# A state space stage: the weighted sums over 16 states, shared between ScalarE, an accumulating transfer and VectorE

## The reference

```python
xz = einsum('bld,ed->ble', x, W_in); u, z = split(xz, 2)
uc = silu(conv3(u) + conv_b)
x_dbl = einsum('blh,eh->ble', uc, W_xproj)          # dt part (64), B (16), C (16)
dt = softplus(einsum('blr,hr->blh', dtp, W_dt) + b_dt)
A = -exp(A_log)
def step(h, (u_t, dt_t, B_t, C_t)):
    dA = exp(dt_t[:, None, :] * A[None, :, None])
    h = dA * h + B_t[:, :, None] * u_t[:, None, :]
    y_t = einsum('bn,bnh->bh', C_t, h)               # the sum over 16 states
y = (scan(step) + D * uc) * silu(z)
out = einsum('blh,dh->bld', y, W_out)
```

## Time and profile before

| | |
|---|---|
| median of 3 runs | 3569.99 us (3563.14 to 3570.53) |
| span of the profiled execution | 3547.4 us |
| what lies around the span (median less span) | 22.6 us |
| DVE, PE, POOL, ACT busy, 200 to 800 us | 591.5, 533.8, 523.9, 472.0 us |
| the stage | 0 to about 910 us |

### The profile page before, as it was taken

How to read it: one execution, slowest core, us unless ns; L and a number is a source line. 1 busy time by engine, 2 the same in 40 slices (tenths; PEclk the granted TensorE clock), 3 DMA queues, 4 the chain that set the end, 5 groups by cost and what they waited for, 6 DMA issues and landing times. The chain is left out here.

```text
span 3547.4 us, 59663 instructions
## 1 busy us (share of the span) xinstructions
PE 3336.7 (94%) x21120; PEld 2437.0 (69%) x21120; DVE 2409.3 (68%) x5247; ACT 1564.9 (44%) x3124; POOL 1736.2 (49%) x2205
## 2 busy tenths in 40 slices
PE   7888988888589999999999989999999999999999
PEld 5666666666468888888876656666655566666565
DVE  8999999999655555555554447777733377777332
ACT  6887778876242222222221125555511255555111
POOL 6988889888450000000012237777611277777221
PEclk9999999999789999999999999999999999999999
DMA  4011101111441000010012211112121111121121
GB/s 143 1 62 62 62 1 62 62 56 46 146 125 37 13 10 13 10 37 12 12 36 74 81 60 37 37 37 60 30 74 54 60 32 38 37 72 31 61 65 35
DMA packets 166972, 176.13 MB, mean 50 GB/s; under 512 B 22756, under 2 KB 150264, under 8 KB 166296
## 3 DMA queue, kind: packets, MB, share of 16 engines
q1 hardware_dynamic: 163272, 162.94, 14.2%
q0 software_dynamic: 3408, 9.38, 0.7%
HBM read 94.19 MB, written 78.09 MB: 49 GB/s over the span
## 5 line engine op out<-in xcount | busy, mean ns | idle before, releaser
L3087 ACT ACTIVATE win_probs<-win_sc,win_nbias,tile_rn 128x256 f32<-128x256 f32 x512 | 282.3, 561 | 311.7 <-DVE win_nbias L3171 311.7
L438 POOL TENSOR_TENSOR ssm_acc<-ssm_acc,ssm_weighted 128x512 f32<-128x512 f32 x255 | 339.0, 1339 | 101.4 <-ACT ssm_weighted L587 100.7
L424 POOL TENSOR_SCALAR ssm_ub<-ssm_uT,ssm_bcT 128x512 f32<-128x512 f32 x512 | 359.1, 725 | 21.8 <-PE ssm_pu L1151 18.0
L1151 PEld LDWEIGHTS ssm_pu<-ident,ssm_ub 128*128 128x128 f32 x2048 | 237.6, 142 | 184.9 <-issue 87.0
L3273 PE MATMUL win_pa<-win_w_wqkv,tile_hT 128*128 128x512 f32 x744 | 360.9, 622 | 0.0
L1151 PE MATMUL ssm_pu<-ident,ssm_ub 128*128 128x128 f32 x2048 | 308.4, 279 | 51.0 <-DVE ssm_state L821 33.8
L1998 POOL TENSOR_TENSOR lin_rstd<-lin_mv,lin_eps 128x1 f32<-128x1 f32 x30 | 5.7, 190 | 667.5 <-DVE lin_mv L173 667.5
L1167 PE MATMUL ssm_pt<-ident,ssm_state 128*128 128x128 f32 x2040 | 278.1, 278 | 48.4 <-DVE ssm_acc L831 30.3
L821 DVE TENSOR_TENSOR_SCAN ssm_state<-ssm_da,ssm_carry,ssm_pu 128x512 f32<-128x512 f32 x256 | 312.5, 1261 | 2.3 <-ACT ssm_da L575 2.3
L2689 PE MATMUL glu_up<-block_hT,glu_w_w 128*128 128x512 f32 x704 | 305.7, 592 | 3.4 <-DVEq L88 3.4
L821 DVE TENSOR_TENSOR_SCAN ssm_state<-ssm_da,ssm_pu 128x512 f32<-128x512 f32 x256 | 296.8, 1200 | 4.9 <-PE ssm_pu L1151 2.7
(11 more groups left out here) (422 smaller groups left out, 7399.4 us busy)
## 6 DMA issues: line engine op xcount, KB each, us to landing
sorted_rows<-block_zeros SPq DMA_DIRECT2D x8, 4290.0 KB, 15.8
block_wide<-x SPq DMA_DIRECT2D x18, 512.0 KB, 6.6
tile_raw<-in_tables SPq DMA_DIRECT2D x64, 128.0 KB, 2.2
a<-tile_y SPq DMA_DIRECT2D x64, 128.0 KB, 1.7
block_wide<-a SPq DMA_DIRECT2D x32, 256.0 KB, 3.3
block_x<-a SPq DMA_DIRECT2D x16, 512.0 KB, 5.3
block_x<-sorted_rows SPq DMA_DIRECT2D x39, 130.0 KB, 2.6
x<-block_more SPq DMA_DIRECT2D x16, 256.0 KB, 2.2
```

Source lines behind the costliest of these rows:

```text
L424: nc.gpsimd.tensor_scalar(ub[:, i % 2, t, :], uT[:, k % 2, t, :], bcT[:, k % 2, t, n:n + 1], 1.0, ALU.mult, ALU.mult).then_inc(ub_ready.se ...
L438: nc.gpsimd.tensor_tensor(acc[:, k % 2, t, :], acc[:, k % 2, t, :], weighted[:, j, :], ALU.add)\
L1151: last = nc.tensor.transpose(pu[c][:, t * P:(t + 1) * P], ub[:, i % 2, t, c * P:(c + 1) * P], ident)
L3087: nc.scalar.activation(probs[:, head, :], sc[j][:, r, :], ACT.Exp, bias=nbias[:, g, j, r:r + 1], scale=rn[:, turn.side, 0, head:head + 1], ...
```

## The change

VectorE keeps only tile 0 of each state (`add_first`). ScalarE weighs tiles 1, 2 and 3 into one of two buffers of 128x1536 (`weighted[i % 2]`); one of them lies in `yn`, whose rest holds `xd`. For each state GpSimd issues one transfer, SBUF to SBUF, which adds the 128x1536 buffer to `acc` (tiles 1 to 3) while it writes. It waits for the transfer of the state before, and a weighing waits for the transfer of the state two back. The last state of the last block is summed by VectorE alone, three adds more (`add_last`). TensorE waits for those who now empty its banks. `work` moves into the convolution's buffer `u`, so the column that an odd block takes over from its left neighbour (`keep_left`) is copied before the softplus, right after the SiLU. The load of the expert bias moves from the end of this stage into the next one.

```diff
@@ state_space_stage, buffers and counters
+        work = u[:, :, 1:BLK + 1]
-        xd = s.sb("xd", [XR, BLK])
+        weighted = [memory.spare[:, 0:(TB - 1) * HID].rearrange("p (t h) -> p t h", h=HID), s.sb("weighted", [P, TB - 1, HID])]
+        xd = memory.spare[0:XR, (TB - 1) * HID:(TB - 1) * HID + BLK]
-        weighted = s.sb("weighted", [P, 2, HID])
...
@@ gpsimd
-            def add_odd(i, j):
-                k, t = i // NS, 2 * j + 1
+            def add_weighted(i):
+                k = i // NS
                 if i % NS == 0:
                     pool.wait_ge(begun.sem, begun.at(k))
-                pool.wait_ge(weighed.sem, weighed.at(i, j + 1))
-                pool.wait_ge(sums_odd.sem, sums_odd.at(i - 1, j + 1))
-                nc.gpsimd.tensor_tensor(acc[:, k % 2, t, :], acc[:, k % 2, t, :], weighted[:, j, :], ALU.add)\
-                  .then_inc(sums_odd.sem, 1)
+                pool.wait_ge(weighed.sem, weighed.at(i))
+                if i:
+                    pool.wait_ge(added.sem, added.at(i - 1))
+                nc.gpsimd.dma_start(acc[:, k % 2, 1:TB, :], weighted[i % 2][:, :, :], accum_op=ALU.add).then_inc(added.sem, 16)
...
@@ scalar
-            def weigh(i, j):
-                k, t = i // NS, 2 * j + 1
-                act.wait_ge(state_turned.sem, state_turned.at(i, 2 * j + 2))
-                act.wait_ge(sums_odd.sem, sums_odd.at(i - 1, j + 1))
-                nc.scalar.activation(weighted[:, j, :], turned_bank(i, t)[:, :], ACT.Copy,
+            def weigh(i, t):
+                k = i // NS
+                act.wait_ge(state_turned.sem, state_turned.at(i, t + 1))
+                if t == 1 and i >= 2:
+                    act.wait_ge(added.sem, added.at(i - 2))
+                nc.scalar.activation(weighted[i % 2][:, t - 1, :], turned_bank(i, t)[:, :], ACT.Copy,
                                      scale=bcT[:, k % 2, t, NS + i % NS:NS + i % NS + 1]).then_inc(weighed.sem, 1)
...
                 if 0 <= i - 1 < N * NS - 1:
-                    weigh(i - 1, 1)
+                    weigh(i - 1, 2)
+                    weigh(i - 1, 3)
...
@@ vector
+            def add_first(i):
                 if i % NS == 0:
-                    dve.wait_ge(begun.sem, begun.at(k, t + 1))
+                    dve.wait_ge(begun.sem, begun.at(i // NS, 1))
+                dve.wait_ge(sums_first.sem, sums_first.at(i - 1))
+                weigh_and_add(i, 0).then_inc(sums_first.sem, 1)
...
             def add_last():
+                i = N * NS - 1
+                dve.wait_ge(added.sem, added.at(i - 1))
+                for t in range(1, TB):
+                    weigh_and_add(i, t).then_inc(sums_last.sem, 1)
...
-                if behind:
-                    add_even(i - 1, 1)
...
@@ tensor, transpose_state
+                if t < 2:
+                    pe.wait_ge(weighed.sem, weighed.at(i - 1, t + 2))
+                elif i == N * NS - 1:
                     pass
+                elif t == 2:
+                    pe.wait_ge(sums_first.sem, sums_first.at(i))
                 else:
+                    pe.wait_ge(weighed.sem, weighed.at(i, 1))
...
@@ MoeStart
-        sp.dma_start(self.m.expert_b[:, :], w["expert_b"].partition_broadcast(P)).then_inc(self.experts_in, 16)
     def load_experts(self, sp):
+        sp.dma_start(self.m.expert_b[:, :], self.w["expert_b"].partition_broadcast(P)).then_inc(self.experts_in, 16)
         sp.wait_ge(self.wide_free, 16 * 2 * TB)
```

More of the change, by code:

```diff
@@ L202, in state_space_stage @@
         s = Scope(nc, ctx, tag)
-        w_in, x, h0, hT, uc, work, gatedT, out = (memory.w_in, memory.x, memory.n, memory.hT_all, memory.uc, memory.work,
-                                                  memory.gatedT, memory.half_y)
+        w_in, x, h0, hT, uc, gatedT, out = (memory.w_in, memory.x, memory.n, memory.hT_all, memory.uc, memory.gatedT,
+                                            memory.half_y)
         x_after, h_after = memory.tile_y[0:1, 0, :], memory.tile_y[0:1, 1, :]
@@ L265, in state_space_stage @@
         state_turned = s.counter("state_turned", per=TB, credit=2)
-        sums_even, sums_odd = s.counter("sums_even", per=2, credit=1), s.counter("sums_odd", per=2, credit=1)
-        weighed = s.counter("weighed", per=2, credit=1)
+        sums_first, weighed = s.counter("sums_first", credit=1), s.counter("weighed", per=TB - 1, credit=1)
+        added, sums_last = s.counter("added", per=16), s.counter("sums_last", per=TB - 1)
         carried = s.sem("carried")
@@ L652, in decays, with keep_left @@
                 act.wait_ge(decay_ready.sem, decay_ready.at(0))
+            def keep_left():
+                nc.scalar.activation(u[:, :, 0:1], u[:, :, BLK:BLK + 1], ACT.Copy).then_inc(left_ready.sem, 1)
             def silu_first(c):
@@ L683, in _ @@
             silu_first(3)
+            keep_left()
             nc.scalar.preload_act_table_set("natural_log_exp_and_others")
@@ L700, in _ @@
                     step_decay(i + 1, 0)
-                if 0 <= i - 1 < N * NS and (i - 1) % NS != 7:
-                    weigh(i - 1, 0)
+                if 0 <= i - 1 < N * NS - 1 and (i - 1) % NS != 7:
+                    weigh(i - 1, 1)
                 second_product(i - 1)
@@ L1064, in transpose_sum @@
                 if c == 0:
-                    pe.wait_ge(sums_even.sem, sums_even.at(k * NS + NS - 1))
-                    pe.wait_ge(sums_odd.sem, sums_odd.at(k * NS + NS - 1))
+                    pe.wait_ge(sums_first.sem, sums_first.at(k * NS + NS - 1))
+                    if k == N - 1:
+                        pe.wait_ge(sums_last.sem, sums_last.at(0))
+                    else:
+                        pe.wait_ge(added.sem, added.at(k * NS + NS - 1))
                 if k == N - 1 and c >= 2:
@@ L1158, in transpose_state @@
                         pe.wait_ge(z_copied.sem, z_copied.at(0))
-                j = t // 2 + 1
-                if i == N * NS - 1 and j == 2:
-                    pass
-                elif t % 2:
-                    pe.wait_ge(weighed.sem, weighed.at(i, j - 1) if j == 2 else weighed.at(i - 1))
+                if t < 2:
+                    pe.wait_ge(weighed.sem, weighed.at(i - 1, t + 2))
+                elif i == N * NS - 1:
+                    pass
+                elif t == 2:
+                    pe.wait_ge(sums_first.sem, sums_first.at(i))
                 else:
-                    pe.wait_ge(sums_even.sem, sums_even.at(i, j - 1) if j == 2 else sums_even.at(i - 1))
+                    pe.wait_ge(weighed.sem, weighed.at(i, 1))
                 for c in range(CT):
@@ L2308, in __init__ @@
         self.scores, self.attnT = xs[:, :].rearrange("p (h t) -> p h t", t=P), yn[:, 0:TB * D].rearrange("p (r t) -> p r t", t=P)
-        self.uc, self.work = channels(xs), channels(yn)
+        self.uc, self.spare = channels(xs), yn
         self.w_in, self.experts, self.expert_b = weights(add), weights(wide), yn
```

39 lines of the change are left out of this document (15 added, 24 removed).

## The result

The changed kernel takes 3620.16 us (median of 4, 3617.28 to 3622.21), the kernel before beside it 3569.47 us (median of 4, 3563.14 to 3570.53). The ratio is 1.0146, interval [1.0132, 1.016]: 50.7 us slower. The forecast was 25 us faster; the rival in which the transfer paces the stage is what happened, at less than its price.

A forecast was written before the change was run, and what follows sets the result against it. VectorE (DVE), nine tenths or more busy, bounds the state space stage. -81 + 33 + 12 - 8 + 12 + 12 + 3 + 1 = -16 us, 9 taken back for overlap: -25 us, 3545 us, range 3515 to 3562.

The forecast's parts named there:

- the rival in which the transfer paces the stage: State space stage: issue to landing exceeds the step, so all but heavy steps take that long; 3650 us, chance 0.38.
- About 2 us a block: Transfer of sums, landing taken as 6.0 us: bare steps don't hide it, ACT-bound steps do; +12 us for 8 blocks.
- 7.7 - L is in hand: Bare steps: L is the transfer's issue to landing; 7.7 us pass before ACT's wait two states on.
- slack in one group helps another in nothing: Step groups of a block: engine order is fixed in code, so idle time in steps 0 to 6 doesn't help 10 to 15.
- - 9: Stage: late ACT steps hide late transfers after a clearing, so two losses overlap; 9 us taken back.
- DVE, -81: Stage: VectorE has 126 fewer adds at the packed spacing of 0.64 us; -81 us.
- ACT, +33 and +12: ScalarE's third weighing: +33 us from steps 10 to 15 over 7 blocks, +12 from steps 7 to 9 over 8.
- POOL and the convolution, -8: DVE's 56 convolution adds: fewer POOL reads let most run at 0.724 us in place of 0.858; -8 us.
- Clearings, +12: Six clearings of 4290 KB in the stage: two transfers of sums share the queues with each; 2 us six times, +12 us.
- The end, +3: Stage end: last transfer starts about when the last scan ends, lands 6 us on, then three adds; +3 us.
- 13 L + 25.7: Rival's block length: 13 steps at issue-to-landing time L, three heavy steps 25.7 us together; even with before at 6.4 us.

The follow-up runs named there:

- one tile: Changed kernel whose transfer adds tile 1 alone (256 KB in place of 768); tiles 2 and 3 are weighed but never added: 3526.04 us.
- a copy's 3.5: Changed kernel whose transfer copies the same 768 KB over the sums in place of adding them: 3531.45 us.
- the split: Changed kernel, whole computation, POOL adding tile 1 by its own instruction, the transfer adding tiles 2 and 3 (512 KB): 3559.72 us, ratio 1.0017.
- the first profile: Changed kernel, nothing altered, its first profiled execution: 3622.14 us, stage end 969.4.
- the second: Changed kernel again, nothing altered, on another chip: 3608.78 us, ratio 1.0166; stage end in its profile 965.5.
- the clearings first: Changed kernel with all eight clearings of the sorted rows issued at the start of the stage, none in the loop: 3601.05 us.
- split with pieces: The split with each of the six clearings in the loop cut into eleven pieces, one a step: 3556.87 us, ratio 0.997.
- the run that broke up the four: Split with pieces, POOL's order changed to two scalings of u, addition of tile 1, two scalings, transfer issue: 3572.04 us, ratio 1.0015.

## Why the prediction was wrong

**The step that failed** is the transfer: "At 6.0 the ACT-bound steps (38.1/6 = 6.35 us) hide it", "About 2 us a block", with "7.7 - L is in hand". The landing was right (5.7 for 6.0). What was wrong is what it was compared with. First, the period of the chain is landing and the next issue, 6.2 us, against bare steps of 5.1 to 6 us (as they are with one tile), so each of them uses up some of what is in hand; the 77 waits of POOL for the transfer before say that it is not won back. Second, the heavy steps do not hide it. The prediction took 6.35 us as a step's even length in steps 10 to 15, but the steps there are uneven: with one tile they take 5.5, 5.9, 7.3, 7.7, 5.7 and 6.9 us in the block shown, three of six under the period. Weighings are met in the order of the code, a late transfer holds the weighing two states on (ACT waited 70 us for transfers), and with it TensorE and the scans. The prediction itself had written that slack in one group helps another in nothing, and then averaged within a group. The runs: with the landing at 3.2 us the stage ends at 890.8, with a copy's 3.5 at 895.0, with 4.5 (the split) at 924.2, with 5.7 at 969.4 and 965.5.

**What the loss is made of.** This goes by the first profile, 969.4; in the second everything between it and the run with one tile is 4 us less. Forecast for the stage without the transfer's losses: -81 + 33 + 12 - 8 = -44. The nearest run (one tile) has 890.8 - 913.3 = -22. The rest, 969.4 - 890.8 = 79 us, was forecast at +12 + 12 + 3 - 9 = 18. By where it lies: blocks 1 to 6, 57 us; block 0, 5; block 7, 10; the tail, 8. Clearings in the loop beside the long transfer make some 35 of it (blocks 1 to 6, 117.6 against 111.5 us with the clearings first), the chain by itself the other 44.

- *DVE, -81.* Neither shown nor refuted as a spacing; with ACT's weighings as before and a small transfer 48 us arrive (913.3 - 865.2). Much of the rest is that steps 10 to 15 were near ACT's limit before, which the prediction has in its ACT term.
- *ACT, +33 and +12.* Steps 10 to 15: predicted about 38 us, measured 39.1 (one tile) and 38.0 (split with pieces): right. Steps 7 to 9: predicted 19.4, measured 20.8. The third weighing by itself costs 26 us, or 10 to 15 where the transfer hides a part; the 45 forecast contain what steps 10 to 15 lack already with two.
- *POOL and the convolution, -8.* The 56 additions took 55.3 us in all before (mean 987 ns) and take 61.3 now (mean 1095, the row below): wrong in sign, by 14 us. Their least, median and most are 719/752/3240 ns against the earlier trace rows: the median fell as expected, the tail doubled. With one tile in the transfer they take 717/751/1137 and 46.9 us in all, 8.4 less than before. So the term came true where the chain does not pace; in part by luck, since it was worked out from the median (858) and a sum follows the mean. The row of the changed kernel in the grouped lines, 60 to 900 us, then DVE and POOL side by side (two timelines, 537 to 543 us):
```profile
L771 DVE SCALAR_TENSOR_TENSOR block_wide<-ssm_u,ssm_conv_w,block_wide 128x512 f32<-128x512 f32 x56 | 61.3, 1095 | 1.0
```
```profile
538.29 4.02 DVE L771 SCALAR_TENSOR_TENSOR block_wide<-ssm_u,ssm_conv_w,block_wide 128x512 f32<-128x512 f32 x2
```
```profile
537.39 0.88 POOL L440 DMA_DIRECT2D ssm_acc<-block_yn  x1 [2.60 <-DMA ssm_acc<-ssm_weighted]
538.00 2.97 POOL L425 TENSOR_SCALAR ssm_ub<-ssm_uT,ssm_bcT 128x512 f32<-128x512 f32 x4
```
  The two additions last as long as POOL's four scalings back to back and then run. Released by the landing, POOL has no gap for them. That POOL's reads hold them up is a reading of these lines and not shown: the run that broke up the four changed more than this and still has additions of up to 4.86 us. Nor is a landing needed for it, as the 4.5 us of the split show.
- *Clearings, +12.* A size, 35 in place of 12: two transfers of sums are late behind each burst (steps 10 and 11), and of the 7.6 us that the prediction worked out for the two it let 2 stand, the others being in hand or hidden by ACT; with the period at 6.2 us there was nothing in hand.
- *The end, +3.* 8.5 us: "starts about when the last scan ends" was wrong, since the last transfer waits for the one before (issued 955.51, with 5.7 us landed at about 961.2).
- *The rival* had the mechanism and nearly the break-even: "even at L = 6.4 us". Its formula, 13 L + 25.7, gives 106.3 us a block for the measured period of 6.2, so faster than before; measured were 110 to 113 without clearings (mean 111.5), 1.5 us more than before on that chip (110.0). The heavy steps, which it left as they are, are not spared. Its condition, L above 6.4, did not come (5.7); the chain paced all the same. Its chance of 0.38 was already above the forecast's 0.36, and the formula alone would not have made it larger.

## What to carry to other kernels

A transfer that must wait for its forerunner is an engine with one instruction per step: count its period (landing and next issue) and compare it with the shortest steps, not with the mean, and count every other transfer on the queues as its competitor. Before an addition goes into a transfer, ask whether a smaller transfer is enough: here two tiles of three, with the large clearing cut in pieces, turned +1.5% (+1.7% on a second chip) into -0.3%. And an idle DMA share says nothing of a chain of transfers, which is bound by the time from issue to landing (here 5.7 us each, with DMA shares of 0.57 to 0.79).

## What the runs showed of the hardware

- Accumulating from SBUF into SBUF, issued by POOL: 256, 512 and 768 KB land in 3.2, 4.5 and 5.7 us; a plain copy of 768 KB in 3.5. So some 1.2 us per 256 KB and 2 us fixed, an estimate from these three. The estimate of 5.6 us by the Trainium skill ("DMA: Bandwidth & Descriptors", Anatomy of one DMA, with "Collectives: The Full Stack", The bandwidth ceiling) agrees with the 5.7. POOL is held 0.88 us by each issue, 0.59 by that of the copy.
- TensorE lost its full clock for moments beside waits that come from the late chain. Timeline and windows of 4 us of the changed kernel:
```profile
574.20 0.60 PE L1175 MATMUL ssm_pt<-ident,ssm_state 128*128 128x128 f32 x4
577.23 1.12 PE L1175 MATMUL ssm_pt<-ident,ssm_state 128*128 128x128 f32 x4 [2.43 <-ACT ssm_weighted L587]
```
```profile
572.00:576.00 4.00, 2.80 (x17) 1.63 (x15) 3.44 (x4) 1.18 (x3) 0.00 (x0) 1.00 1.01 254
576.00:580.00 4.00, 2.77 (x6) 1.22 (x6) 1.45 (x2) 3.51 (x7) 3.06 (x5) 0.54 1.05 323
580.00:584.00 4.00, 4.00 (x22) 3.56 (x21) 1.68 (x3) 2.17 (x5) 1.05 (x2) 0.61 0.51 102
584.00:588.00 4.00, 4.00 (x30) 3.24 (x30) 3.44 (x4) 4.00 (x7) 3.06 (x5) 1.00 0.84 172
```
  Round a wait of 2.43 us without work (574.8 to 577.2) the granted clock goes from 1.00 to 0.54 and 0.61 of full in the 8 us from 576 on, so mostly at the lower of its two levels, 1.2 GHz, and four transposes take 1.12 us in place of 0.60. In the window 200 to 800 us it was 0.95 against 0.99 before and 1.00 with one tile. So a wait on a transfer can cost more than itself; how much of the 44 us this is, no run here separates.
- Clearings of 4290 KB land in 15.5 us in the kernel before, 20.3 beside the chain, 42.7 with eight at once.

Not tried: the 768 KB transfer without its wait for the one before, which would separate the order from the length (the runs above change only the length); two alternating chains into separate sums; and one transfer for each tile.
